# Four-layer sequence model on one core: where the halved second products of a batch's last expert stand in TensorE's order

## What is computed

```python
for e in range(E):
    h = jax.nn.gelu(context_c @ ew1[e] + eb1[e], approximate=True)
    y = h @ ew2[e] + eb2[e]
    out = out + w_be[:, e][:, None, None] * mask[e][None, :, None] * y
shared = jax.nn.gelu(context_c @ sw1 + sb1, approximate=True) @ sw2 + sb2
return out + shared
```

## Time and profile before

| | |
|---|---|
| median of 3 runs | 2287.81 us (2287.75 to 2288.5) |
| the profiled execution | 2287.28 us |
| its span, first to last instruction | 2285.5 us |
| PE matmuls busy | 2171.6 us (95%) |
| PE weight loads busy | 1417.5 us (62%) |
| DVE busy | 1549.0 us (68%) |
| ACT busy | 1235.7 us (54%) |
| POOL busy | 560.5 us (25%) |
| mean granted TensorE clock | 0.993 |

### The profile page before, as it was taken

How to read it: one execution, slowest core, us unless ns; L and a number is a source line. 1 busy time by engine, 2 the same in 40 slices (tenths; PEclk the granted TensorE clock), 3 DMA queues, 4 the chain that set the end, 5 groups by cost and what they waited for, 6 DMA issues and landing times. The chain is left out here.

```text
span 2285.5 us, 93941 instructions
## 1 busy us (share of the span) xinstructions
PE 2171.6 (95%) x38552; PEld 1417.5 (62%) x38552; DVE 1549.0 (68%) x7281; ACT 1235.7 (54%) x4360; POOL 560.5 (25%) x1178
## 2 busy tenths in 40 slices
PE   8899999999999999999988699999999999999999
PEld 6677777777777777777763246464646555463666
DVE  5777777778777787777774776684848476675620
ACT  4555555555555555555556465756565565656422
POOL 0222122232212322223223132221213132222100
PEclk9999999999999999999999799999999999999999
DMA  4111111101000000010001323231221323222020
GB/s 121 32 41 36 39 32 39 48 21 36 25 27 30 27 30 20 30 32 26 16 28 54 78 85 83 88 74 65 64 94 47 84 88 83 88 56 88 1 88 10
DMA packets 111007, 117.28 MB, mean 51 GB/s; under 512 B 69604, under 2 KB 92516, under 8 KB 106484
## 3 DMA queue, kind: packets, MB, share of 16 engines
q1 hardware_dynamic: 107172, 108.75, 15.9%
q10 hardware_dynamic: 3408, 2.52, 0.4%
HBM read 75.53 MB, written 21.04 MB: 42 GB/s over the span
## 5 line engine op out<-in xcount | busy, mean ns | idle before, releaser
L137 PE MATMUL psFI<-wh,Hs 128*8 128x128 f32 (+3 forms) x8192 | 324.6, 276 | 60.5 <-DVE Hs L252 47.1
L137 PE MATMUL psOR<-wh,RH 128*16 128x128 f32 (+3 forms) x8320 | 321.4, 272 | 2.2 <-ACT RH L340 2.0
L137 PEld LDWEIGHTS psFI<-wh,Hs 128*8 128x8 f32 (+3 forms) x8192 | 182.2, 99 | 178.6 <-DVE Hs L252 178.6
L2050 ACT ACTIVATE pexp<-bank 128x1024 f32<-128x1024 f32 x256 | 246.2, 1022 | 55.4 <-PE bank L1374 55.4
L340 ACT ACTIVATE RH<-RT 128x16 f32<-128x16 f32 x512 | 110.8, 216 | 261.2 <-DVE RT L256 261.2
L1265 PE MATMUL bank<-x3T,ew 128*128 128x512 f32 x512 | 238.0, 592 | 0.0
L236 DVE STREAM_TRANSPOSE FIT<-psFI 128x128 f32<-128x128 f32 x512 | 162.2, 317 | 100.7 <-PE psFI L137 98.2
L331 ACT ACTIVATE sFI<-FIT 128x32 f32<-128x32 f32 x512 | 118.6, 232 | 200.0 <-DVE FIT L236 195.0
L137 PEld LDWEIGHTS psOR<-wh,RH 128*16 128x16 f32 (+1 forms) x8320 | 205.7, 104 | 4.7 <-ACT RH L340 3.7
L137 PE MATMUL psG<-wh,Hs 128*8 128x64 f32 (+3 forms) x8192 | 208.3, 219 | 0.0
L1964 ACT ACTIVATE W_wf<-bank,eb1s 128x512 f32<-128x512 f32 x128 | 87.5, 684 | 166.8 <-PE bank L1265 164.3
(11 more groups left out here) (369 smaller groups left out, 4144.7 us busy)
## 6 DMA issues: line engine op xcount, KB each, us to landing
ew<-in_ew SPq DMA_DIRECT2D x32, 1024.0 KB, 7.6
qkv_scratch<-qkvr SPq DMA_DIRECT2D x31, 384.0 KB, 2.9
big<-qkv_scratch SPq DMA_DIRECT2D x7, 1536.0 KB, 6.7
XX<-in_xT SPq DMA_DIRECT2D x31, 256.0 KB, 2.7
x_scratch<-xr SPq DMA_DIRECT2D x32, 128.5 KB, 2.6
x<-x_scratch SPq DMA_DIRECT2D x8, 514.0 KB, 4.3
ada<-ada_scratch SPq DMA_DIRECT2D x8, 512.0 KB, 7.3
out_x<-x SPq DMA_DIRECT2D x7, 512.0 KB, 3.4
```

The source lines that it names most:

```text
L137: last = pe.matmul(bank[32 * j:32 * j + width, :], state(k), weights[:, k, j, cols], start=False, stop=k == KC - 1, tile_position=(0, 32 * ...
L2050: up(act.activation(M.pexp[:, n % 2, 2 * pr:2 * pr + 2, :], M.PS[pr][:, :, :], ACT.Exp, scale=1.0 / math.sqrt(HD)), "exps")
```

## The change

In `tensor_round` the half products of steps 18 and 19 leave the loop over the steps and stand behind `up(23)`. The eight quarters of steps 20 to 23 on tiles 0 and 1 are dealt to units 0 to 3 as 4, 2, 1 and 1, where each unit had two. From unit 4 on nothing is changed, and no instruction is added or left out.

```diff
+    first_halves = [(i, q) for i in range(HALVES, STEPS) for q in FIRST_HALF]
     second_halves = [(i, q) for i in range(WHOLE, STEPS) for q in SECOND_HALF]
+    behind = [first_halves[0:4], first_halves[4:6], first_halves[6:7], first_halves[7:8]] + [second_halves[n:n + 1] for n in range(12)]
...
                 down(i - LEAD - 1)
             if i >= LEAD and i % FC != LEAD and (i - LEAD < WHOLE or e == NB - 1):
                 down(i - LEAD)
-            elif WHOLE <= i - LEAD < HALVES:
-                down_in_half(i - LEAD, FIRST_HALF)
...
-            if e >= 1 and n < STEPS - HALVES:
-                down_in_half(HALVES + n, FIRST_HALF, e - 1)
-            elif e >= 1:
-                i, q = second_halves[n - (STEPS - HALVES)]
-                down_in_half(i, (q,), e - 1)
+            if e >= 1:
+                for i, q in behind[n]:
+                    down_in_half(i, (q,), e - 1)
...
         if experts:
             steps(FC + LEAD + 4, STEPS)
+            for i in range(WHOLE, HALVES):
+                down_in_half(i, FIRST_HALF)
```

## The result

The changed kernel takes 2275.14 us (median of 6 runs, 2274.59 to 2278.04), the kernel before 2288.99 us beside it (6 runs, 2287.75 to 2290.77). The ratio is 0.9944 with a 95% interval of 0.9934 to 0.9955: faster by 10 to 15 us. 2275.3 us was forecast, from 2287.81 us as the time before.

What follows compares the result with a forecast made beforehand. PE was taken to bound every round, so only its standing still could be saved: 6 x 1.92 + 0.94 = 12.46, rounded to 12.5 us, from 2287.81 us to 2275.3 us. The range was 2274.2 to 2277, stretched to 2280.0 us (78%).

Steps and rivals of the forecast that it cites:

- The turn: Before the transposes, PE's wait on the last gelu goes, hidden behind two half products: 0.94 us at each of 7 turns.
- Unit 0: In the attention's first unit, PE's wait on the exponentials before the next scores goes: 1.00 us at 6 attentions.
- ACT's gap: ACT would idle about 0.4 us between the exponentials of unit 0 and unit 1, where before there was none.
- Units 1 to 3: Unit 1 keeps 2.59 us, units 2 and 3 take 2.17 each; values of unit 3 start 1.92 us earlier per turn.
- The tie between PE and ACT: In units 2 and 3, ACT's exponentials and PE are both ready for the second pair of scores after 2.44 us.
- The sum: Whole kernel: 1.92 us at six turns plus 0.94 at the turn into round 8, 12.46 us, giving 2275.3 us.
- One-quarter units held by ACT: Rival: units 2 and 3 stay at 2.59 us, so the gain is 7.4 us, 2280.4 us; chance 7%.
- ACT's way as the bound: Rival: ACT's 1.41 us from gelu to copy were twice as long; gain 7.9 us, 2279.9 us; chance 4%.
- Room on PE: Rival: PE does not bound the stretch between two attentions, so the gain is swallowed: 0, 2287.8 us; chance 8%.
- First products that catch up with the gelus: Rival: a late gelu of step 21 holds `up(23)` and all behind it; 8.1 us slower, 2295.9 us; chance 3%.

Runs made afterwards that it cites:

- deal 8, 0, 0, 0: The changed kernel with all eight quarters in unit 0 and none in units 1 to 3: 2279.32 us, ratio 0.9962 to the kernel before.

## Why the prediction was right

**The turn.** 0.94 us at each of 7 turns was forecast, with the transposes right behind the half products. They follow at once, and in the seventh turn too. `up(23)` did not wait for a gelu: the three first products run without a gap.

**Unit 0.** 1.00 us was to go at 6 attentions, by exponentials that end 2.60 and 3.52 us after the transposes start. They start at 1431.52, which makes 2.47 and 3.40 us, and four quarters bring PE there at 3.44 and 3.71. The copy comes 0.97 us after the transposes start, where the prediction took about 1.1 and named no row for it. The values of unit 0 come 3.97 us after the transposes (4.02 forecast); the 0.05 us are in the transposes, which take 0.97 us to the scores when they follow without a wait and took 1.02 in the earlier trace rows. ACT's gap of 0.47 us was put at 0.4.

**Units 1 to 3.** 2.59 + 2 x 2.17 was forecast, 2.59, 2.21 and 2.17 were measured. The tie between PE and ACT holds, as PE waits for no exponential there; deal 8, 0, 0, 0 shows what a unit takes when PE is on the short side of it.

**The sum.** 1.92 us a round for 1.94 measured, and 12.46 us in all for 6 x 1.94 + 0.94 = 12.6. The median came out at 2275.14 for 2275.3. That the 0.16 us agree so well is luck: the runs of one kernel scatter over 3 us, the forecast started from 2287.81 us where the kernel before came out at 2288.99, and the medians differ by 13.85 us where 12.46 was forecast and six rounds and a turn make 12.6. The 1.94 is not luck.

**The rivals.** One-quarter units held by ACT: refuted by units of 2.21 and 2.17 us, which lie at the tie but not behind it. ACT's way as the bound, and with it the longer switch that the Trainium skill gives ("ScalarE: Activation LUTs", What ACT_TABLE_LOAD costs: 2.66 us): refuted where nothing hides it, by 1.42 us from gelu to copy with one half product behind, and by 1.5 us for each of three switches in a row. Room on PE: one more `up` cost all of its 1.72 us. With it goes what the Trainium skill ("Perfetto Trace Analysis", Identifying the Most-Contended Engine) says of the share of weight loads, which was 64% in that stretch: it does not tell the headroom for fp32 products of 128x512 here. The start of one group to the start of the next does. First products that catch up with the gelus: no such wait showed.

What the prediction did not say is that its two waits are not independent. The 0.94 and the 1.00 are right as shares of the whole, but not as what each part of the change brings. Alone they bring 1.32 and 0.82.

## What to carry to other kernels

Where an in-order engine that bounds the kernel waits at a turn from one stage to another, look for work elsewhere in its order whose inputs are long ready, and put it behind the last piece that the other engine waits for. How much is not the length of the wait: 0.94 us stood still, and one half product (0.86 us) was 0.3 us a round slower than two (1.72), three (2.58) 0.7 us slower. What has to be covered is ACT's way. From the end of `up(23)` to its copy that is 0.20 + 0.69 + 1.41 = 2.30 us by the earlier trace rows, of which the transposes cover 0.97, so that by this estimate 1.33 us are wanted. Work out from one turn when each engine would be ready, and trust the distance from turn to turn more than the median when the effect is near the scatter of the runs. Two waits with one late engine behind them are one lateness, and their gains alone do not add up.

## What the runs showed of the hardware that I had not expected

- On PE a quarter of 128x128 fp32 products between scores (64 rows of the array) and values (32 columns), in whichever order, takes 0.63 us for 0.43: its first entry takes 0.32 us and its last 0.31, for 0.22 each among its like. From values to scores it costs nothing that can be seen (1.00 us in deal 8, 0, 0, 0). Behind transposes the same quarter takes 0.53 us (1449.24 to 1449.78 in the changed kernel), as only its last entry is dearer; 0.06 us are then paid by the first transpose.
- A wait of PE of 1.64 us and one of 0.52 after it were followed by a stretch with a lower granted clock (0.88 over 14 us) at three of six turns, every second one, for 1.5 us each. This is from one run.
- Until 1420 us the same program took 3.4 us more in one execution than in another. 2.8 us of it arise in two stretches of 10 us in which the granted clock was lower (0.72 for 0.83, 0.82 for 1.00). That the clock is the cause of all of it was not shown by a run.
